# Layer-norm statistics: the combination of means and variances moved from VectorE to GpSimd

## The reference

```python
def _layernorm(x, axis=-1, eps=1e-05):
    m = jnp.mean(x, axis=axis, keepdims=True)
    v = jnp.var(x, axis=axis, keepdims=True)
    return (x - m) / jnp.sqrt(v + eps)
...
    x = x + _L0_attn_ref(_layernorm(x, axis=-1), ...)   # norm 0: 16 heads of 8, softmax over 512 tokens
    x = x + _L0_ffn_ref(_layernorm(x, axis=-1), ...)    # norm 1: silu(x Wg) * (x Wu), hidden 384, then down
    x = x + _L1_attn_ref(_layernorm(x, axis=-1), ...)   # norm 2: q and k are rms-normed per head
    x = x + _L1_ffn_ref(_layernorm(x, axis=-1), ...)    # norm 3: base matmul + gated low-rank experts
    return x
```

## Time and profile before

| what | us |
|---|---|
| median of 3 runs | 1890.0 (1884.27 to 1898.27) |
| profiled execution, its own time | 1890.93 |
| its span, first to last instruction | 1889.1 |
| TensorE busy | 1730.6 (92%) |
| VectorE busy | 1596.9 (85%) |
| ScalarE busy | 1423.2 (75%) |
| GpSimd busy | 438.8 (23%) |
| mean granted TensorE clock | 0.981 of full speed |

### The profile page before, as it was taken

One profiled execution on the slowest core, in us unless ns is written; L12 is line 12 of the kernel. 1 busy time (PEld: TensorE's weight loads), 2 busy tenths in 40 slices (PEclk: granted clock), 3 DMA queues, 4 the chain that ended last, 5 costly groups with the idle time before them and its releaser, 6 DMA issues.

```text
span 1889.1 us, 32181 instructions
## 1 busy us (share of the span) xinstructions
PE 1730.6 (92%) x10958; PEld 651.8 (35%) x10958; DVE 1596.9 (85%) x3587; ACT 1423.2 (75%) x2921; POOL 438.8 (23%) x579
## 2 busy tenths in 40 slices
PE   3999899999999999999999999999999999999895
PEld 1233233434233343333334333333433334333233
DVE  3988899898998989888898989889899897797981
ACT  2687778787877878777787877878787786777772
POOL 3122122131222313113132221213221221312211
PEclk9999999999999999999999999999999999999996
DMA  6232414233050422305042150613315042122310
GB/s 123 59 84 52 125 31 127 51 86 92 25 148 24 120 58 79 99 23 150 25 114 58 59 125 14 156 27 86 86 40 143 14 129 43 37 63 75 81 36 23
DMA packets 162644, 141.34 MB, mean 75 GB/s; under 512 B 38761, under 2 KB 144050, under 8 KB 162482
## 3 DMA queue, kind: packets, MB, share of 16 engines
q1 hardware_dynamic: 162482, 139.29, 28.8%
HBM read 77.38 MB, written 55.57 MB: 70 GB/s over the span
## 4 chain that ended last, share of the span: by engine, by line
PE 49%; DVE 24%; ACT 16%; issue 5%; DMA 4%; POOL 1%; SPq 1%; DVEq 0%; ACTq 0%; POOLq 0%
DVE neg_max L911 16%; PE ps L1205 14%; PE ps L1190 10%; ACT probs L707 9%; PE ps L1226 7%; PE ps L1180 5%; PE ps L1219 3%; PE ps L1231 3%; PE ps L1143 2%; PE ps L1270 2%; ACT xn L713 2%; DMA k_stack<-k_rows 2%; DVE bn L887 1%; ACT kf L736 1%; DVE qk L972 1%
## 5 line engine op out<-in xcount | busy, mean ns | idle before, releaser
L911 DVE TENSOR_REDUCE neg_max<-ps 128x1 f32<-128x512 f32 x2048 | 1309.4, 681 | 137.6 <-PE ps L1180 131.9
L707 ACT ACTIVATE probs<-ps 128x512 f32<-128x512 f32 x2048 | 1105.1, 600 | 282.5 <-PE ps L1190 279.6
L1180 PE MATMUL ps<-k_stack,q_stack 48*128 48x512 bf16 x2048 | 701.4, 390 | 54.9 <-DVE neg_max L911 35.6
L1190 PE MATMUL ps<-q_stack,k_stack 50*128 50x512 bf16 x2048 | 670.5, 386 | 35.5 <-ACT probs L707 27.1
L1205 PE MATMUL ps<-probs,v_aug 128*32 128x512 f32 x4096 | 552.6, 612 | 1.3 <-ACT probs L707 0.5
L1190 PEld LDWEIGHTS ps<-q_stack,k_stack 50*128 50x128 bf16 x2048 | 155.8, 94 | 609.4 <-ACT probs L707 367.9
L1180 PEld LDWEIGHTS ps<-k_stack,q_stack 48*128 48x128 bf16 x2048 | 161.8, 93 | 215.6 <-DVE neg_max L911 155.2
L606 POOL TENSOR_TENSOR o_raw<-o_raw,rden_all 128x512 f32<-128x512 f32 x64 | 81.3, 1270 | 367.7 <-DMA rden_all<-rden_rows 367.6
L587 POOL TENSOR_TENSOR rstd<-vpe,half_neg 128x4 f32<-128x4 f32 x64 | 64.4, 1007 | 335.2 <-DVE vpe L902 335.2
L1205 PEld LDWEIGHTS ps<-probs,v_aug 128*32 128x32 f32 x4096 | 81.0, 108 | 141.0 <-issue 99.8
L713 ACT ACTIVATE xn<-x,shift,rstd 128x128 f32<-128x128 f32 x192 | 81.3, 494 | 27.9 <-POOL shift L589 27.9
(11 more groups left out here) (103 smaller groups left out, 1493.2 us busy)
## 6 DMA issues: line engine op xcount, KB each, us to landing
q_stack<-q_rows SPq DMA_DIRECT2D x128, 192.0 KB, 4.3
k_stack<-k_rows SPq DMA_DIRECT2D x128, 192.0 KB, 5.4
rden_all<-rden_rows SPq DMA_DIRECT2D x64, 256.0 KB
q_rows<-qp SPq DMA_DIRECT2D x32, 384.0 KB, 2.6
k_rows<-kp SPq DMA_DIRECT2D x32, 384.0 KB, 2.8
q_rows<-qp SPq DMA_DIRECT2D x32, 256.0 KB, 2.9
k_rows<-kp SPq DMA_DIRECT2D x32, 256.0 KB, 2.9
x_in<-in_L_attn_x SPq DMA_DIRECT2D x16, 256.0 KB, 3.4
```

The source lines that it names most:

```text
L707: act.activation(probs[:, g % RING, :], home("score", (l, b, u)), ACT.Exp).then_inc(exps, 1)
L911: dve.tensor_reduce(neg_max[l][:, pair // 2, col:col + 1], home("max", (l, b, n)), AX.X, ALU.max, negate=True).then_inc(max_taken, 1)
L1180: pe.matmul(home("max", (l, b, m)), q_stack[l][row:row + KROWS, pair, tok:tok + 128], k_stack[l][row:row + KROWS, pair, :], start=True, st ...
L1190: pe.matmul(home("score", (l, b, u)), k_stack[l][row:row + AROWS, pair, tok:tok + 128], q_stack[l][row:row + AROWS, pair, :], start=True, ...
```

## The change

VectorE keeps bn_stats alone. The steps `moments` and `factors_in` are gone with their places in the tables (mo0 to mo3, fa0, fa3) and their semaphores. GpSimd's `norm_factors` now waits for the statistics themselves (`bn_done`) and computes from the two halves' means m0, m1 and the two halves' sums of squares s0, s1, for all four tiles at once: -m0/2 and -m1/2; s0/128 + eps/2 and s1/128 + eps/2; the gap of the half means; the sum of the two variances; the gap squared; neg_mean as the sum; and vpe = variance + gap squared. Seven instructions on 128x8 or 128x4 operands, ordered by seven steps of one semaphore `factor[k]` (the engine waits for its own results), then the same pow and multiply as before. GpSimd's place in its table (nf0 to nf3) is the same.

```diff
-          "S0": {"st0a": 25, "st0b": 27, "mo0": 33, "fa0": 35},
+          "S0": {"st0a": 25, "st0b": 27},
...
-          "M1": {"add0": 19, "st1": 20, "mo1": 20, "gm0": 31, "gm1": 34, "gm2": 37, "down": 44, "st2": 45,
-                "mo2": 45, "tqa": 54, "tqb": 54, "nw0": 55, "nw1": 61, "nw2": 64, "nw3": 65, "nw4": 65,
+          "M1": {"add0": 19, "st1": 20, "gm0": 31, "gm1": 34, "gm2": 37, "down": 44, "st2": 45, "tqa": 54, "tqb": 54, "nw0": 55, "nw1": 61, "nw2": 64, "nw3": 65, "nw4": 65,
...
-          "E": {"add1": 22, "st3a": 22, "st3b": 26, "mo3": 27, "fa3": 28, "ro0": 45, "ro1": 47, "ro2": 49,
+          "E": {"add1": 22, "st3a": 22, "st3b": 26, "ro0": 45, "ro1": 47, "ro2": 49,
...
-                pool.wait_ge(var_ready[k], b + 1)
+                pool.wait_ge(bn_done[k], b + 1)
+                halves = bn[k][:, :, :].rearrange("p t (h c) -> p t h c", h=2)
+                done = N_FACTOR * b
+                pool.tensor_scalar(half_mean[k][:, :, :], halves[:, :, :, 1], -0.5, 0.0, ALU.mult, ALU.add
+                                   ).then_inc(factor[k], 1)
+                pool.tensor_scalar(half_var[k][:, :, :], halves[:, :, :, 2], 1.0 / D, 0.5 * LN_EPS, ALU.mult, ALU.add
+                                   ).then_inc(factor[k], 1)
+                pool.wait_ge(factor[k], done + 1)
+                pool.tensor_tensor(mean_gap[k][:, :], half_mean[k][:, :, 0], half_mean[k][:, :, 1], ALU.subtract
+                                   ).then_inc(factor[k], 1)
+                pool.wait_ge(factor[k], done + 2)
+                pool.tensor_tensor(vpe[k][:, :], half_var[k][:, :, 0], half_var[k][:, :, 1], ALU.add).then_inc(factor[k], 1)
+                pool.wait_ge(factor[k], done + 3)
+                pool.tensor_tensor(gap_sq[k][:, :], mean_gap[k][:, :], mean_gap[k][:, :], ALU.mult).then_inc(factor[k], 1)
+                pool.tensor_tensor(neg_mean[k][:, :], half_mean[k][:, :, 0], half_mean[k][:, :, 1], ALU.add
+                                   ).then_inc(factor[k], 1)
+                pool.wait_ge(factor[k], done + 5)
+                pool.tensor_tensor(vpe[k][:, :], vpe[k][:, :], gap_sq[k][:, :], ALU.add).then_inc(factor[k], 1)
+                pool.wait_ge(factor[k], done + 7)
                 pool.tensor_tensor(rstd[k][:, :], vpe[k][:, :], half_neg[:, :], ALU.pow).then_inc(rstd_ready[k], 1)
...
-            def moments(k, b):
-
-                dve.wait_ge(bn_done[k], b + 1)
-                for t in range(TT):
-                    last = dve.bn_aggr(mv[k][:, t, :], bn[k][:, t, :])
-                last.then_inc(mv_done[k], 1)
-
-            def factors_in(k, b):
-
-                dve.wait_ge(mv_done[k], b + 1)
-                dve.tensor_scalar(neg_mean[k][:, :], mv[k][:, :, 0], -1.0, None, ALU.mult)
-                dve.tensor_scalar(vpe[k][:, :], mv[k][:, :, 1], LN_EPS, None, ALU.add).then_inc(var_ready[k], 1)
```

More of the change, by code:

```diff
@@ L241, in build @@
         bn = [sb(f"bn{k}", [128, TT, 6]) for k in range(4)]
-        mv = [sb(f"mv{k}", [128, TT, 2]) for k in range(4)]
+        half_mean = [sb(f"half_mean{k}", [128, TT, 2]) for k in range(4)]
+        half_var = [sb(f"half_var{k}", [128, TT, 2]) for k in range(4)]
+        mean_gap = [sb(f"mean_gap{k}", [128, TT]) for k in range(4)]
+        gap_sq = [sb(f"gap_sq{k}", [128, TT]) for k in range(4)]
         vpe = [sb(f"vpe{k}", [128, TT]) for k in range(4)]
@@ L327, in build @@
         bn_done = [sem(f"bn_done{k}") for k in range(4)]
-        mv_done = [sem(f"mv_done{k}") for k in range(4)]
-        var_ready = [sem(f"var_ready{k}") for k in range(4)]
+        factor = [sem(f"factor{k}") for k in range(4)]
+        N_FACTOR = 7
         rstd_ready = [sem(f"rstd_ready{k}") for k in range(4)]
@@ L1034, in _ @@
             stats(0, x_in, 0)
-            moments(0, 0)
-            factors_in(0, 0)
             dve.wait_ge(first_loaded, 16 * 6)
@@ L1043, in _ @@
             stats(0, x_in, 1)
-            moments(0, 1)
-            factors_in(0, 1)
             for t in TIMES:
@@ L1077, in _ @@
                     stats(3, x3, b, (2, 3))
[L1078 to L1083, removed]
                 for link in range(3):
@@ L1101, in _ @@
                     stats(0, x_in, b, (2, 3))
[L1102 to L1107, removed]
                 b = at(DVE_DUE, "add0", t)
@@ L1114, in _ @@
                     stats(1, x1, b)
[L1115 to L1118, removed]
                 for c in range(NH):
@@ L1129, in _ @@
                     stats(2, x2, b)
[L1130 to L1133, removed]
                 for half in (0, 1):
```

## The result

The changed kernel took 1906.85 us (median of 7 runs, 1905.28 to 1919.59), the kernel before 1888.63 us on the same chip (7 runs, 1881.56 to 1898.27): a ratio of 1.0113, 95% interval 1.0078 to 1.0147. It is slower by 1.1%. The forecast of 1895 was 12 us too low; the time lies in the forecast's range, and in the case "slower by over 1%" that had 0.13. The profiled execution took 1905.28 us, span 1903.5, against 1889.1: +14.4 us where the forecast's sum had +5.3.

The account below looks back on a forecast made before the run. The chain that ended last was 49% TensorE, 24% VectorE; norm 2's path through GpSimd was taken to decide. +6.0 - 3.6 + 0.6 + 0.6 + 1.7 = +5.3 us on 1890.0 gave 1895, range 1877 to 1911.

Parts of the forecast that it names:

- slower by over 1%: Whole kernel: case of a time more than 1% (18.9 us) slower; chance 0.13.
- within 1%: Whole kernel: case of a time within 1% (18.9 us) of the kernel before; chance 0.82.
- the price of the seven: GpSimd ahead of pow: the seven added instructions make pow 0.6 us later, bounds 0.49 and 1.27.
- Norm 3's wait of 0.26 us: Norm 3: removing bn_aggr between two maxima ends TensorE's wait in 14 elements, 14 x 0.26 = -3.6 us.
- Norm 1's xn still has cover: Norm 1: about 1.9 us of cover in 13 elements, no gain; +0.6 us for elements 0, 14 and 15 together.
- The tail: Norm 3 of element 15: no cover, everything to the output hangs on shift, +0.6 us.
- I put 0 for the six: Norm 2: ten elements pay 10 x 0.6 = +6.0 us; in the other six, 0.59 us of slack swallows the lateness.
- one more drop, +1.7: TensorE's clock: idle time added before norm 2's transposes brings one more drop, +1.7 us.
- (c): TensorE's clock: drops move with the phase, eight fewer or more at 1.7, 1880 or 1907; chance 0.10, half each way.
- (a): GpSimd: every instruction pays its round trip, norm 2 decides in all elements, +28.6, 1919; chance 0.14, 0.12 beyond 1%.
- (b): VectorE: its saved time pays, in full 1852 (chance 0.04) or at the chain's 24% share 1881 (chance 0.13).
- (d): Norm 1: the shared port holds up a VectorE cast and subtraction, 6.4 us on top, 1901; chance 0.03.

Follow-up runs that it names:

- run 2: The kernel before with norm 2 alone moved to GpSimd: 1906.31 us, ratio 1.0095.
- run 1: The changed kernel with norm 2 alone combined on VectorE again; norms 0, 1 and 3 stay on GpSimd: 1890.72 us, ratio 1.0013.
- run 4: The kernel before with four, in a second kernel eight, small GpSimd multiplies ahead of norm 2's pow: 1905.83 and 1918.78 us.
- the second profile of the changed kernel: The changed kernel measured again, beside the filled one: 1910.31 us, ratio 1.0113.
- Run 5: The changed kernel with six identity transposes filling TensorE's gap ahead of norm 2's transposes, on two chips: 1900.16 and 1894.43 us.
- the kernel with gaps of 0.57 us: The kernel before with four small GpSimd multiplies ahead of norm 2's pow, also called the first late kernel: 1905.83 us, ratio 1.0083.
- the one with gaps of 1.18: The kernel before with eight small GpSimd multiplies ahead of norm 2's pow: 1918.78 us, ratio 1.0158.
- run 6: The kernel before without bn_aggr and the two tensor_scalar in all norms, pow and multiply taking constants: 1862.53 us, ratio 0.9861.
- run 3: The kernel before with the seven GpSimd instructions added behind shift in all norms, into tiles nobody reads: 1889.18 us, ratio 0.9999.
- the filled one again: The changed kernel with six identity transposes in TensorE's gap at norm 2, second measurement: 1894.43 us, ratio 1.0040.
- the changed one with either new place: The changed kernel with xn2 at unit 50 and xt2 at 52, or xt2 alone at 52: 1903.83 and 1924.42 us.

## Why the prediction was right, and where not

**In the range, and partly by luck.** The way was right, slower, and so was the place. But the sum gave +5 us where the medians have +18, and the time lies in the range by its upper end, which the rivals had set. The case called the most likely, within 1%, had 0.82, and the ratio of 1.0113 is outside it, though its interval begins at 1.0078.

**Right, with their sizes.** Norm 2 is where the change is decided, and the price of the seven: pow 0.64 us later against 0.6 taken (bounds 0.49 and 1.27). ScalarE's wait 1.23 (forecast "about 1.2"), the gap ahead of the transposes, VectorE's maximum at once behind the statistics. Norm 3's wait of 0.26 us is gone; what that brought isn't shown (run 2). Norm 1's xn still has cover in 13 elements, in most of them 1.27 us instead of 1.92; in elements 0, 14 and 15 its wait grew by 0.65 us and more, and no run shows what of that reached the transposes. The tail paid 0.6. The period without a drop came out at the forecast 111.1. Runs 1 and 2 show the place, run 4 the mechanism.

**Wrong: "I put 0 for the six".** The slack of 0.73 us in the earlier trace rows was not a property of the element. It was there because the clock fell just ahead of those transposes. In the changed kernel the drops near norm 2 come elsewhere; the one of element 6 (pow at 819.60) is this, length and granted clock as in the earlier trace rows:

```profile
823.60:825.20 1.60, 1.51 (x8) 0.88 (x7) 1.43 (x4) 1.60 (x4) 0.00 (x0) 0.87 0.00 0
825.20:826.80 1.60, 1.60 (x5) 1.27 (x4) 1.17 (x5) 0.77 (x2) 0.00 (x0) 0.50 0.07 10
```

Its transposes had started at 822.72, 0.14 us behind xn. So the slack is nowhere, and all 16 elements pay. Counted for all 16, norm 2 would have stood in the sum with 16 x 0.6 = 9.6 us, not 6.0. For norms 2 and 3 together the periods give 16 x 0.30 = 5 us, where the sum had 6.0 - 3.6 = 2.4.

**Mis-sized: the clock, "one more drop, +1.7".** The profiled execution has 13 stretches at the lower level where the one before had 11, the second profile of the changed kernel 18. Over all runs it is some 24 us more at that level, seven drops of 3.4 us, and filling the gap brings back some 12 us, seven drops' worth at 1.7. The prediction had such an amount among its rivals, as (c), 0.05 for the slower half, with the phase as its reason. Run 5 shows that it falls when TensorE's gap is filled. My argument against (c), that "the idle time that the change adds is under a microsecond of a period", is the step that failed most: it took the cost for no larger than the gap. How much of the 12 us is the clock's stays open (experiment 5), and so does the reason for the amount, since the kernel with gaps of 0.57 us paid about as much beyond its lateness as the one with gaps of 1.18.

**The sum by the runs.** 5 us in the periods without a drop, 0.6 in the tail and the 12 that filling the gap brings back make 18 of the 21.4 between the means on the two chips (1909.5 and 1888.1); some 3 us stay without a place. The profiled execution had 14.4, and was the second fastest of the changed kernel's 13 runs.

**Rivals.** (a) fell: only half_var and pow start more than 0.16 us behind the instruction ahead, and pow came 0.64 later, not 1.27. (b) fell for this change: run 1 shows norms 0, 1 and 3 worth nothing, and at norm 2 VectorE's gain turns into idle time, as the prediction had it. It is worth something only together with a shorter chain (run 6). (c) holds in its size; its reason, the phase, wasn't tested by itself, and run 5 speaks for the gap. (d) fell by run 3.

**Open.** Why the clock falls at one place and not at another, and so why the changed kernel has it low at 111 us and at 1797 us. What of the 12 us is the clock's, and how they split between norm 2 and drops elsewhere. Why eight multiplies brought no more beyond their lateness than four, though the clock fell further.

## What to carry to other kernels

Before moving work from a busy engine to an idle one, ask who waits for its result: here 29 us less busy time on VectorE were bought with 0.65 us more in a chain of three engines, and the chain decided. Look for the place where the two paths meet: if they are equally long, a shorter one brings nothing, and a longer one costs its full length in every period. A new gap of TensorE can cost more than its own length; test it by filling it with matmuls that nobody reads. Slack seen only where the clock is low isn't slack.

## What the runs showed of the hardware

- Seven small GpSimd instructions, each 0.20 us whether tensor_scalar on 128x8 or tensor_tensor on 128x4, take 1.32 us from the start of the first to the start of what waits for the last. Two of them as groups, by line:

```profile
L593 POOL TENSOR_SCALAR half_var<-bn 128x8 f32<-128x8 f32 x64 | 12.9, 202 | 5.1
...
L596 POOL TENSOR_TENSOR mean_gap<-half_mean 128x4 f32<-128x4 f32 x64 | 12.9, 202 | 0.0
```

- Its last column is the idle time before them. half_var stands 0.28 us behind half_mean (1153.53 to 1153.81), not 0.15, though the code has no wait between the two; this 0.08 in each of 64 makes up the 5.1. Two of the same form follow each other there; the cause wasn't tried.
- In six of the 14 profiled executions (the first late kernel, the changed kernel again, the filled one again, that of run 1, and the changed one with either new place) one period of twelve lasted 117.5 to 120.6 us, with a stretch of 13.7 to 17.1 us at the lower clock that began some 60 us behind norm 2's pow. It makes that period 6 to 9 us longer. Each kernel has one profile, so what it does to a median isn't known.
- The same code doesn't get the same clock each time: up to its first norm 2 the first late kernel runs the instructions of the kernel before, and had 30.7 us at the lower level there, where the kernel before had none.
